# Attention scores of a Flamingo block: sixteen 32-row products in two row groups in place of four 128-row products against block-diagonal keys

## The reference, cut to what matters

```python
q = (layernorm(x) @ Wq.T + bq).reshape(n, s, 16, 32).transpose(0, 2, 1, 3)
k = (ctx @ Wk.T + bk).reshape(n, 128, 16, 32).transpose(0, 2, 1, 3)
v = (ctx @ Wv.T + bv).reshape(n, 128, 16, 32).transpose(0, 2, 1, 3)
att = jnp.einsum('bhsd,bhtd->bhst', q, k) / sqrt(32)
att = where(pad_mask == 0, -1e9, att); att = where(subsq_mask == 0, -1e9, att)
out = jnp.einsum('bhst,bhtd->bhsd', softmax(att), v)
x = x + tanh(g_xattn) * out
# then a mixture of 8 experts, top 2, and a shared expert, over layernorm(x):
x = x + tanh(g_ffn) * ffn(layernorm(x))
```

## Time and profile before

| | |
|---|---|
| median of 3 runs | 1175.54 us (1173.56 to 1176.14) |
| span of the profiled execution | 1178.0 us |
| PE busy | 1047.6 us (89%), 7335 instructions |
| PE weight loads busy | 673.1 us (57%) |
| DVE busy | 821.4 us (70%) |
| ACT busy | 530.6 us (45%) |
| POOL busy | 442.5 us (38%) |
| score products (L1071), PE busy | 140.4 us in 256 instructions |

### The profile page before, as it was taken

One profiled execution on the slowest core, in us unless ns is written; L12 is line 12 of the kernel. 1 busy time (PEld: TensorE's weight loads), 2 busy tenths in 40 slices (PEclk: granted clock), 3 DMA queues, 4 the chain that ended last, 5 costly groups with the idle time before them and its releaser, 6 DMA issues.

```text
span 1178.0 us, 26603 instructions
## 1 busy us (share of the span) xinstructions
PE 1047.6 (89%) x7335; PEld 673.1 (57%) x7336; DVE 821.4 (70%) x2932; ACT 530.6 (45%) x1041; POOL 442.5 (38%) x655
## 2 busy tenths in 40 slices
PE   5499858999999999870599999999999999999997
PEld 3377747777777787760255555555554444444443
DVE  3899856887888888875276666666665566666666
ACT  1266526666666666651244444444443222223232
POOL 1345526676666666643212222121210332222322
PEclk9699978998999899985699999999999999999999
DMA  5564572334333223422333333333342544545443
GB/s 194 216 224 164 129 181 75 92 91 91 91 103 95 88 97 91 108 95 32 98 118 108 121 111 121 111 118 114 117 124 73 161 158 154 173 142 174 150 162 125
DMA packets 76731, 146.96 MB, mean 125 GB/s; under 512 B 20912, under 2 KB 23088, under 8 KB 73872
## 3 DMA queue, kind: packets, MB, share of 16 engines
q1 hardware_dynamic: 46512, 66.01, 21.1%
q10 hardware_dynamic: 17280, 44.83, 10.6%
q0 software_dynamic: 12896, 35.58, 9.8%
HBM read 94.04 MB, written 52.35 MB: 124 GB/s over the span
## 4 chain that ended last, share of the span: by engine, by line
PE 59%; issue 14%; DVE 10%; POOL 8%; ACT 4%; DMA 2%; POOLq 1%; another core or an unknown queue 1%; DVEq 0%; ACTq 0%; SPq 0%
PE bank L1036 14%; PE bank L1037 14%; PE bank L1038 14%; PE bank L1028 8%; PE bank L1071 4%; DVE arena L768 3%; PE bank L1089 3%; POOL arena L466 2%; POOL token_of_row L502 2%; DVE arena L857 1%; ACT arena L612 1%; DMA token_of_row<-arena 1%; DVE peak L871 1%; PE bank L1102 1%; PE bank L1103 1%
## 5 line engine op out<-in xcount | busy, mean ns | idle before, releaser
L1028 PE MATMUL bank<-ident,arena 128*128 128x128 f32 (+1 forms) x1592 | 188.4, 266 | 89.6 <-DMA arena<-normed_rows,arena 30.0
L1036 PE MATMUL bank<-weights,arena 128*128 (+1 forms) x682 | 260.2, 382 | 2.1 <-ACT arena L654 1.9
L1037 PE MATMUL bank<-weights,arena 128*128 (+1 forms) x682 | 260.2, 381 | 0.0
L1038 PE MATMUL bank<-weights,arena 128*128 (+1 forms) x682 | 259.8, 381 | 0.0
L1028 PEld LDWEIGHTS bank<-ident,arena 128*128 128x128 f32 (+1 forms) x1592 | 160.4, 132 | 137.1 <-issue 100.3
L518 POOL DMA_INDIRECT arena<-normed_rows,arena x71 | 67.4, 949 | 241.8 <-PE bank L1028 227.0
L1089 PEld LDWEIGHTS bank<-arena 128*128 128x128 f32 x1024 | 128.6, 195 | 36.2 <-issue 27.7
L1071 PE MATMUL bank<-arena 128*128 128x512 f32 x256 | 140.4, 654 | 8.5 <-DVE arena L768 6.8
L466 POOL TENSOR_TENSOR arena<-arena 128x512 f32<-128x512 f32 x96 | 101.7, 1060 | 85.0 <-DVE arena L768 73.7
L768 DVE CUSTOM_DVE_ANT_0 arena<-bank,arena 128x128 f32<-128x128 f32 x512 | 116.8, 283 | 17.8 <-PE bank L1071 14.5
L1089 PE MATMUL bank<-arena 128*128 128x33 f32 x1024 | 125.7, 273 | 3.8 <-ACT arena L568 3.8
(11 more groups left out here) (170 smaller groups left out, 1890.5 us busy)
## 6 DMA issues: line engine op xcount, KB each, us to landing
expert_rows<-arena ACTq DMA_DIRECT2D x71, 256.0 KB, 2.1
arena<-in_x SPq DMA_DIRECT2D x64, 256.0 KB, 3.8
weights<-in_w_gu ACTq DMA_DIRECT2D x8, 1024.0 KB, 4.9
x_rows<-arena SPq DMA_DIRECT2D x32, 256.0 KB
normed_rows<-arena SPq DMA_DIRECT2D x32, 256.0 KB, 5.5
normed_transposed<-arena SPq DMA_DIRECT2D x32, 256.0 KB, 2.6
arena<-normed_transposed SPq DMA_DIRECT2D x32, 256.0 KB, 3.2
arena<-x_rows SPq DMA_DIRECT2D x32, 256.0 KB, 3.5
```

Source lines behind the costliest of these rows:

```text
L1028: last = t.transpose(dst[:, c * P:(c + 1) * P], src[:, c * P:(c + 1) * P], (ident16 if src.dtype == F16 else ident)[:, :])
L1036: t.matmul(dst, hi[:, rows], w_hi(c), start=(c == 0), stop=False)
L1037: t.matmul(dst, hi[:, rows], w_lo(c), start=False, stop=False)
L1038: last = t.matmul(dst, lo[:, rows], w_hi(c), start=False, stop=(c == chunks - 1))
```

## The change

The keys are stored once for each head, without zeros (`k_t`, 128 rows by 128 columns for each batch and chunk; head 4c + g is on rows 32g to 32g + 31). The rest of the space is still carved, so that nothing else moves. The scores become 16 products, each with the 32 rows of one head as contraction and 128 key columns. Group k now means the 4 heads 4c + k, one from each chunk, and these go to one bank. `scores(k)` is called for k = 0 and 2 only, and makes groups k and k + 1 in turn, one product for row group k into one bank, one for row group k + 1 into the other. It waits for the maxima of group k - 1. On PE, mix 0 and mix 1 now follow the first scores, and then comes scores(2). The values and the normalised output are indexed by the new order of heads; the output of 8 heads takes two instructions of 4 heads. The clearing of `kbd` goes, and the keys take 4 instructions of 128 rows in place of 16 of 32 rows.

```diff
-        kbd = carve(B * EC * HG * T).rearrange("p (b c n) -> p b c n", b=B, c=EC)
+        k_t = carve(B * EC * T).rearrange("p (b c n) -> p b c n", b=B, c=EC)
+        carve(B * EC * (HG - 1) * T)
...
+        attn_by_group = attn.rearrange("p (c g d) -> p g c d", c=EC, g=HG)
...
-            d.memset(kbd, 0.0).then_inc(kv_set, 1)
-            d.memset(vaug[:, :, :, D:D + 1], 1.0)
+            d.memset(vaug[:, :, :, D:D + 1], 1.0).then_inc(kv_set, 1)
...
-                    for h in range(HG):
-                        rows = slice(h * D, (h + 1) * D)
-                        d.tensor_scalar(kbd[rows, :, c, h * T:(h + 1) * T], bank[c][rows, 0:B * T].rearrange("p (b t) -> p b t", b=B),
-                                        bk_s[rows, c:c + 1], float(D) ** -0.5, ALU.add, ALU.mult)
+                    d.tensor_scalar(k_t[:, :, c, :], bank[c][:, 0:B * T].rearrange("p (b t) -> p b t", b=B),
+                                    bk_s[:, c:c + 1], float(D) ** -0.5, ALU.add, ALU.mult)
...
-                        d.tensor_tensor(attn[:, half * hs * D:(half + 1) * hs * D].rearrange("p (h d) -> p h d", h=hs), av[:, :, 0:D],
-                                        inv.unsqueeze(2).to_broadcast([P, hs, D]), ALU.mult).then_inc(attn_done[half], 1)
+                        for g in (2 * half, 2 * half + 1):
+                            at = (g % 2) * HG
+                            last = d.tensor_tensor(attn_by_group[:, g], av[:, at:at + HG, 0:D],
+                                                   inv[:, at:at + HG].unsqueeze(2).to_broadcast([P, HG, D]), ALU.mult)
+                        last.then_inc(attn_done[half], 1)
...
-                        need(pe, max_done, group(n, k - 2))
-                        t.matmul(bank[2 + k % 2][:, :], q_t[u][:, k * P:(k + 1) * P], kbd[:, u, k, :],
-                                 start=True, stop=True).then_inc(s_done, 1)
+                        need(pe, max_done, group(n, k - 1))
+                        for c in range(EC):
+                            for g in (k, k + 1):
+                                rows = slice(g * D, (g + 1) * D)
+                                mm = t.matmul(bank[2 + g % 2][:, c * T:(c + 1) * T], q_t[u][rows, c * P:(c + 1) * P],
+                                              k_t[rows, u, c, :], start=True, stop=True)
+                                if c == EC - 1:
+                                    mm.then_inc(s_done, 1)
...
-                                            vaug[:, u, k * HG + h, :], start=True, stop=True)
+                                            vaug[:, u, h * HG + k, :], start=True, stop=True)
...
                 scores(0)
-                scores(1)
                 mix_values(0)
+                mix_values(1)
                 scores(2)
-                mix_values(1)
-                scores(3)
```

## The result

The changed kernel takes 1199.45 us (median; 1196.87 to 1202.04), the kernel before 1175.84 beside it. The ratio is 1.0199, 95% interval 1.0175 to 1.0223: slower by 2%. The prediction was 1197 and slower. The number was right, but by another sum than the one predicted, as the profile shows at once.

The account below looks back on a forecast made before the run. Bound by a ring of scores, maxima, POOL, ACT, q_t and transposes: 1178.0 - 5.9 (start) + 16 (loop) + 11 (written-out iterations) + 2.5 (normalising) = 1201.6, less 2 for the clock and 2.5 from span to median: 1197; range 1170 to 1217.

Parts of the forecast that it names:

- Ring and waits: Loop: scores(0) of v = 1, maxima, POOL, ACT, q_t, transposes wait on each other; PE idles about 1.2 us before scores(2).
- The price of the lateness: Loop: maxima 2 come 1.55 us later in v = 1 and pass it round the ring; +16 us for ten loop steps.
- The price of a call: Score products on PE: 16 pairs of load and matmul take 1.75 us, at least 1.62 if loads go one after another.
- rival 1: Score calls: both row groups run side by side, loads too, 0.9 us a call; 1172, or 1184 with drains; chance 0.27.
- rival 2: PE, idling at scores(2), drops to 1.2 GHz for a call in one of two iterations; 1215; chance 0.13.
- 2 us off for the clock: PE ahead of v = 1: a later v = 0 shortens idle time after which it ran at the lower clock; -2 us.
- granted clock well under 0.96: Sign against the prediction: PE's granted clock from 200 to 510 us falls well under 0.96.
- a call of 1.1 us or less: Sign against the prediction: a call of score products on PE takes 1.1 us or less.
- A loop step: Two iterations of the loop: 30.3 us forecast in place of 28.7; staying at 28.7 would make the prediction wrong.
- The start: Key writes on DVE ahead of PE's first transposes: 1.98 us in place of 7.91, a gain of 5.9 us.
- Normalising: Output on DVE in two instructions of 128 columns: +0.08 us for each half, +2.5 us in all.
- The change between 128-row and 32-row products: PE, four times a tile: a change of tiling mode costs 0 to 0.33 us each; taken as 0.

Follow-up runs that it names:

- e10_together: e8_full with the two loops of a call exchanged back, so both row groups end together at the end of a long call; 1211.21 us, ratio 1.0290.
- e4_outer: The changed kernel with a call's two loops exchanged: 4 products of row group k, then 4 of k + 1; 1229.01 us, ratio 1.0428.
- e3_order: The kernel before, with its four 128-row products, given only the changed order and wait; 1177.38 us, ratio 0.9997.
- e8_full: e4_outer with all 128 rows in each of its 16 products and block-diagonal keys made as in the kernel before; 1186.77 us, ratio 1.0108.
- e5_single: The changed kernel with 32-row products, but one row group a call and the order and waits of the kernel before; 1242.74 us, ratio 1.0586.
- e9_start: The kernel before with half of its 16 key blocks written by ScalarE beside VectorE's half; 1172.85 us, ratio 0.9967.
- e6_keys: The changed kernel with its keys written by 16 instructions of 32 rows in place of 4 of 128; 1204.84 us, ratio 1.0261.

## Why the prediction came out right

**Ring and waits.** Who waits for whom was right. PE waits at scores(2) in nearly every iteration (33.2 us in 30 times between 40 and 530 us, 1.1 each where 1.2 was forecast), and DVE waits for scores. The price of the lateness, 16 us for ten loop steps, is not borne out. e10_together cost 1.8%, 21 us, where 20 to 26 were expected, but a good part of that goes with its lower clock, and its two loop steps at full clock are late by 1.3 and 0.3 us, not by 1.5 to 1.6.

**The price of a call: the step that failed.** The prediction took 1.75 us and said that loads one after another bound it from below at 1.62. A call takes 1.16 us to the end of its last, 1.09 to the next row. The spacing of the mix loads, 0.10 us, is that of loads which all use the same rows; it says nothing of loads for different rows. The spacing of e4_outer's calls, 1.71 us for 16, is near it. The rule of the Trainium skill that the prediction quoted ("TensorEngine Tiling (Array Packing)", Key Properties, tiles load and multiply in parallel) held, and rival 1 was true in this. With a call of 1.1 us the lateness of the ring shrinks to little at full clock, and rival 1 gave 1172.

**The clock: rival 2, wrongly argued, took its place.** The prediction gave it 0.13, since scores behind 1.27 and 2.14 us of idle time had run at full clock. That evidence was of 128-row products, and the sum took 2 us off for the clock. It held for them still in e3_order and e8_full (0.97 to 0.98), less so in e10_together with its longer waits (0.93), but the lower clock follows the 32-row form, even with no idle time at all (e5_single, 0.81). The forecast condition "granted clock well under 0.96" that would make the prediction wrong came true, and so did the one on a call of 1.1 us or less (1.09 to the next row). A loop step took 29.9 us, neither 28.7 nor the 30.3 forecast. That the time came out within 3 us is luck: the prediction had the calls too long and next to nothing for the clock, and the two errors nearly cancel.

Roughly for one iteration of the loop: two calls of 1.1 in place of 1.72 us save 1.2; 32% in place of 8% of about 14.6 us at half speed costs 1.8; the wait at scores(2) adds 0.95; the idle time ahead of the v = 1 transposes, 1.5 every second iteration, mostly goes, 0.7. Together +0.85, measured +0.71. PE's own account over iterations 12 to 31 agrees: its busy time grew from 13.47 to 13.92 us an iteration, its idle time from 0.75 to 1.01.

**The start.** 4 instructions took 1.66 us, not 1.98, and PE begins 6.3 us sooner, against 5.9 forecast. e9_start shows that such a gain can reach the end in the kernel before, and e6_keys suggests it for the changed one; the changed kernel has lost as much again by iteration 12. Its clock is 0.80 from 60 to 200 us, but that this is the cause there was not tested.

**Normalising.** Two instructions take 0.49 us as one row against 0.42: 0.07, as the 0.08 taken.

**The change between 128-row and 32-row products.** The prediction bounded it by 0 to 0.33 us and took 0. At full clock 12 transposes take 1.46 us to the start of a 32-row call (306.89 to 308.35) and 1.34 to that of a 128-row one (301.06 to 302.40): some 0.1 us for one change, or 0.4 a tile if all four cost the same.

**Open.** What e10_together would take with the clock of e8_full, and how much of the 5.2 us behind iteration 32 is the clock, was not tried. No run separates the 32 rows from the tiling that comes with them.

## What to carry to other kernels

Small products in different row groups ran side by side here, loads included, when neighbours in the instruction stream were in different groups; a bound taken from loads that share rows didn't hold for them. But a sum of busy time at full clock isn't the price: compare the granted clock of the stretch with that before, and test a form with the same number of products at full height before believing that idle time is the cause. And when a step's products are made together, ask when the first reader can start, not when the call ends: the same wait was free with the first group at half a call, and with both at its end the kernel took 1.8% longer, in part through the clock.

## What the runs showed of the hardware

- 16 pairs of float32 loads and matmuls of 32 rows by 128 columns took 1.16 us in two alternating row groups and 1.71 us in one group after the other; 16 pairs of 128 rows took 1.95 us with one bank after the other (e8_full) and in turn (e10_together).
- With the same number and order of instructions and the same waits, the granted clock was 0.82 with 32-row and 0.97 with 128-row score products; in e5_single PE was busy without a gap for 310 us at 0.81. The Trainium skill, "TensorE: Matmul & The Clock Gate", section "Why this matters for your kernels", names gaps in TensorE's work as what brings the lower clock back; in e5_single it came back without a gap, and the measurement decides.
- A change from 128-row to 32-row products cost some 0.1 us at full clock (1.46 against 1.34 us for the 12 transposes ahead of a call).
